# One reciprocal over all four groups in the cross-attention of a six-layer transformer stage, with the order of turns derived anew

## What is computed

```
def _L1_xcond_ref(x, noise_emb, context, src_mask, ctx_mask, ...):
    NL, D, H, DFF = (6, 128, 16, 512)
    ...
    def _attn(q, k, v, mask):
        scores = jnp.einsum('bqhd,bkhd->bhqk', q, k) / np.float32(np.sqrt(HD))
        scores = jnp.where(mask[:, None, None, :], jnp.float32(-jnp.inf), scores)
        w = jax.nn.softmax(scores, axis=-1)
        return jnp.einsum('bhqk,bkhd->bqhd', w, v)
    ...
    for i in range(NL):
        xn = _adaln(x, noise_emb, n1_w[i], n1_b[i])
        qkv = xn @ qkv_w[i].T
        ...
        a = _attn(q, k, v, src_mask).reshape(B, L, D) @ so_w[i].T
        x = x + a
        xn = _adaln(x, noise_emb, n2_w[i], n2_b[i])
        ...
        a = _attn(q, k, v, ctx_mask).reshape(B, L, D) @ co_w[i].T
        x = x + a
        xn = _adaln(x, noise_emb, n3_w[i], n3_b[i])
        h = jax.nn.gelu(xn @ f1_w[i].T + f1_b[i], approximate=False)
        x = x + (h @ f2_w[i].T + f2_b[i])
```

## Time and profile before

| | |
|---|---|
| time, median of three | 5061.23 us (5058.92 to 5063.93) |
| the profiled execution | 5061.74 us, span 5059.6 us |
| PE busy in the span | 4376.1 us (86%) |
| DVE busy | 3535.1 us (70%) |
| ACT busy | 2299.6 us (45%) |
| POOL busy | 376.5 us (7%) |
| the transformer stage | from 2121 to 3658 us, PE at a granted clock of 0.85 |

### The profile page before, as it was taken

One profiled execution on the slowest core, in us unless ns is written; L12 is line 12 of the kernel. 1 busy time (PEld: TensorE's weight loads), 2 busy tenths in 40 slices (PEclk: granted clock), 3 DMA queues, 4 the chain that ended last, 5 costly groups with the idle time before them and its releaser, 6 DMA issues. The chain is left out here.

```text
span 5059.6 us, 88974 instructions
## 1 busy us (share of the span) xinstructions
PE 4376.1 (86%) x25446; PEld 2749.6 (54%) x25446; DVE 3535.1 (70%) x17626; ACT 2299.6 (45%) x7385; POOL 376.5 (7%) x306
## 2 busy tenths in 40 slices
PE   8999999999999998488888888888623888997979
PEld 6888888888888886323333333333312553333456
DVE  7888888888888885476677777777445783443435
ACT  4555555555555553145555555555321112332313
POOL 0000000000000000201111111111001001221000
PEclk9999999999999998688888888888755897998679
DMA  0000000000000001222222222222000010000001
GB/s 28 2 2 2 2 2 2 2 2 2 2 2 2 2 2 30 56 53 45 49 45 49 45 49 45 49 45 47 15 8 0 29 34 14 9 7 13 17 1 38
DMA packets 82323, 106.79 MB, mean 21 GB/s; under 512 B 26095, under 2 KB 75434, under 8 KB 79915
## 3 DMA queue, kind: packets, MB, share of 16 engines
q1 hardware_dynamic: 81899, 101.85, 8.4%
HBM read 70.74 MB, written 30.26 MB: 20 GB/s over the span
## 5 line engine op out<-in xcount | busy, mean ns | idle before, releaser
L287 DVE CUSTOM_DVE_ANT_0 I-219junk<-I-215encw,I-218expo,I-227rec 128x77 f32<-128x77 f32 x3072 | 941.6, 357 | 6.2
L1315 DVE TENSOR_REDUCE I-41383nmax<-ps 128x1 f32<-128x512 f32 x768 | 501.4, 685 | 220.2 <-PE ps L984 213.6
L1203 ACT ACTIVATE I-41386prob<-ps 128x512 f32<-128x512 f32 x768 | 428.4, 596 | 229.8 <-PE ps L1021 227.1
L265 ACT ACTIVATE I-217tanh_s<-ps 128x77 f32<-128x77 f32 x1024 | 241.3, 236 | 595.5 <-PE ps L245 595.5
L245 PEld LDWEIGHTS ps<-I-212hist,I-49small 128*128 128x128 f32 x2048 | 305.0, 188 | 297.9 <-DVE I-212hist L323 297.8
L245 PE MATMUL ps<-I-212hist,I-49small 128*128 128x77 f32 x2048 | 456.6, 305 | 0.1
L251 PE MATMUL ps<-I-217tanh_s,I-49small 128*128 128x77 f32 x2048 | 454.5, 304 | 0.0
L984 PE MATMUL ps<-I-41377kS,I-41376qS 96*128 96x512 bf16 x768 | 332.1, 459 | 125.0 <-DVE I-41383nmax L1315 57.8
L247 PE MATMUL ps<-I-212hist,I-216uh_h 128*128 128x128 f32 x2048 | 439.9, 296 | 0.0
L252 PE MATMUL ps<-I-212hist,I-49small 128*128 128x128 f32 x2048 | 439.8, 296 | 0.0
L273 ACT ACTIVATE I-223hh<-I-229gate_t,I-228pre,I-222rh 128x1 f32<-128x1 f32 x1024 | 395.3, 386 | 84.5
(11 more groups left out here) (502 smaller groups left out, 7799.5 us busy)
## 6 DMA issues: line engine op xcount, KB each, us to landing
I-41376qS<-parts SPq DMA_DIRECT2D x24, 768.0 KB, 7.6
parts<-I-41395room SPq DMA_DIRECT2D x36, 384.0 KB, 2.5
parts<-I-41395room SPq DMA_DIRECT2D x36, 256.0 KB, 2.2
I-41377kS<-parts SPq DMA_DIRECT2D x12, 768.0 KB, 7.9
parts<-I-41395room SPq DMA_DIRECT2D x36, 128.0 KB, 1.8
I-49small<-in_layers SPq DMA_DIRECT2D x6, 768.0 KB, 9.0
I-41376qS<-I-41385mrow SPq DMA_DIRECT2D x192, 2.0 KB
I-41376qS<-I-41392crow SPq DMA_DIRECT2D x192, 2.0 KB
```

The lines of the kernel that those rows point to most:

```text
L287: return e.tensor_tensor_reduce(junk[:, 2 * g + b, :], encw[:, g, b, :], expo[:, b, :], inv[:, b:b + 1], rec[:, b, g:g + 1], ALU.mult, ALU ...
L1203: e.activation(prob[:, tau % 2, j, :], k.ps[:, b, :], ACT.Exp, scale=scale).then_inc(free[b], 1)
L1315: e.tensor_reduce(nmax[:, U % HG, i, j:j + 1], k.ps[:, use[0], :], AX.X, ALU.max, negate=True).then_inc(free[use[0]], 1)
```

## The change

It does three things. In the cross-attention all four groups are added on POOL (three additions), one reciprocal serves them, and the second reciprocal is gone. The multiplication of group 3 goes from DVE to POOL, after that of group 1. `cV` has the zero columns that this needs (six more MEMSETs, once, while the stage loads). And the five strings of `TURNS` are new (that of the self-attention's steps included, whose own arithmetic stays).

```
 e.wait_ge(s.zeroed, 2)
 for dst in (V, cV):
     for g in range(HG):
-        for n in range(HG - 1):
-            if n != g and g < HG - 1:
+        for n in range(HG):
+            if n != g and (dst is cV or n < HG - 1 and g < HG - 1):
                 e.memset(dst[:, :, 4 * g:4 * g + 4, 8 + n:9 + n], 0.0).then_inc(s.ones, 1)
...
     n = HG * (r - B) + g
     if g == 0:
-        e.wait_ge(s.csum, 2 * (r - B + 1))
+        e.wait_ge(s.csum, 3 * (r - B + 1))
         e.reciprocal(cinv[:], cinv[:]).then_inc(s.cinv, 1)
         yield
-    if g == HG - 1:
-        e.wait_ge(*done(R[r, ("a", g)]))
-        e.wait_ge(s.cwide, n)
-        e.reciprocal(cinv[:], co_in[:, g, :]).then_inc(s.cinv, 1)
-    e.wait_ge(s.cinv, 2 * (r - B) + 1 + g // (HG - 1))
+    e.wait_ge(s.cinv, r - B + 1)
     if n >= 2:
         e.wait_ge(s.cnormed, n - 1)
     e.stream_shuffle(cwide[:, g % 2, :], cinv[:], [8 + g] * 32).then_inc(s.cwide, 1)
-    if g != 1:
+    if g % 2 == 0:
...
-for g in range(1, HG - 1):
+for g in range(1, HG):
     e.wait_ge(*done(R[r, ("a", g)]))
     if g > 1:
-        e.wait_ge(s.csum, 2 * (r - B) + g - 1)
+        e.wait_ge(s.csum, 3 * (r - B) + g - 1)
         e.tensor_tensor(cinv[:], cinv[:], co_in[:, g, :], ALU.add).then_inc(s.csum, 1)
...
-e.wait_ge(s.cwide, N + 2)
-e.wait_ge(s.cnormed, N + 1)
-e.tensor_tensor(co_in[:, 1, :], co_in[:, 1, :], cwide[:, 1, :], ALU.mult).then_inc(s.cnormed, 1)
-yield
+for g in (1, 3):
+    e.wait_ge(s.cwide, N + g + 1)
+    e.wait_ge(s.cnormed, N + g)
+    e.tensor_tensor(co_in[:, g, :], co_in[:, g, :], cwide[:, g % 2, :], ALU.mult).then_inc(s.cnormed, 1)
+    yield
```

Of the strings, one line shows the kind of change (the middle part of DVE's; the rest has the same form):

```
-        "mmmrmmmmmrmmmmrraaaraaarrrmmmmrmrmrmmmmmmmmmmmmmmmmrrrrrrrrrmrrrrrmrrrrrmrmmmmmmmmmmmmrmrrmrmmrmmrmmrmmmmmmmm"
+        "mmrmmmmmmrrrraaaaaarmrrmmmmrmrmrmmmmmmmmmmmmmmmmmmmmrrrrrrrrrrrrrrrrrmrrrmmmmmmmmmmmmmmmmmmmrrrmrrmmmmrmrmmmmm"
```

79 lines of the change are left out of this document (39 added, 40 removed).

## The result

The changed kernel takes 5106.67 us (median of six runs, 5091.97 to 5124.38), the kernel before, run beside it, 5060.07 (six runs, 5036.54 to 5072.70). The ratio is 1.0097, with a 95% interval of 1.0069 to 1.0126: slower by one per cent. The forecast was 5091.6 in 5040 to 5118, slower with a chance of 0.58. The profiled execution took 5109.62 us with a span of 5107.9, 48.3 more than that of the kernel before.

The account below looks back on a forecast made before the run. No engine fills a piece; the ring of waits between streams bounds it. 2.7 - 1.6 - 1.3 - 0.7 + 4.0 = +3.1 us a piece, nine times, plus 1.9 at the last: 5061.7 + 30 = 5091.6, range 5040 to 5118.

Parts of the forecast that it names:

- E: Self-attention rounds 8 to 15: splits gathered before round 10's last exponential lengthen the stretch, +4.0 us a piece.
- rounds keep up: Rival at ACT, rounds 9 to 11: rounds keep up while splits run, -0.5 us or less there, total 5049; chance 0.25.
- A: Self-attention output product to first cross-attention maxima: four more units of m, bound by DVE's reduces, +2.7 us a piece.
- B: Cross-attention's maxima: three reduces of m moved ahead of it, -1.6 us a piece, bounds -2.05 and 0.
- D: Cross-attention's output product to round 8: two reduces of m where five stood, -0.7 us a piece.
- C: Cross-attention normalisation, fourth group's copy to output product's end: a chain of 13.0 us against 14.3, -1.3 a piece.
- POOL beside DVE: Normalisation, port shared with DVE: POOL's full-tile steps taken at 1.27 us, not stretched, by the earlier trace's row.
- What was taken as nothing: First pieces and a = 11, where only two streams run: 0, with 4 us either way in all.
- rival 3: Five last rounds of a piece: PE idles, granted clock falls to 0.50, +6 us a piece, total 5143; chance 0.08.
- DMA: Where pieces meet: q lands about 5 us before the norm, ending the 3.98 us PE gap; alone this saves nothing.

Follow-up runs that it names:

- e1: One reciprocal (new arithmetic) with the order of the kernel before, the reciprocal two units of m later at r = 12: 5115.81 us, ratio 1.0104.
- e2: The changed kernel's order with the old arithmetic of two reciprocals: 5158.51 us, ratio 1.0189.
- e9: e5 with the changed kernel's tail order (first norm to round 15, r = 3 to 11): 5103.53 us, ratio 1.0099.
- e10: e5 with four units of m put ahead of the first L1094 in seven pieces: 5080.48 us, ratio 1.0039.
- e12: e11 with two units of m behind the maxima, and in r = 2 a round before the first output product: 5053.14 us, ratio 0.9989.
- e11: e5 with r = 12 reordered on PE and the maxima's copy earlier on ACT in four r: 5056.82 us, ratio 1.0000.
- e5: One reciprocal in the old order, changed only from the last product with the values to the output product's end: 5063.46 us, ratio 1.0013.

## Why the prediction was right, and where it was not

- **The time and its sign** were right: 5106.67 in 5040 to 5118, slower as forecast. Of +46.6 us the sum had 30, and the miss was within the range by width, not by reasoning: nine pieces took 1.2 us each more than forecast, the start and the end of the stage 15 more, and the unchanged part behind it happened to be 7 shorter. The reason given was half of the matter: the expected gain of the arithmetic and the expected price of the order were taken as two things that stand side by side. e1 and e2 show that they are one.
- **E** (+4.0 forecast, +4.1 measured) had the place and the size right, and e9 shows the tail's order by itself (+4.1 between rounds 8 and 15, +4.6 a piece). The sum has some luck in it. Rounds 8 to 10 were forecast at 14.4 us and took 11.3 and 14.3 by turns, 12.8 in the mean; rounds 10 to 15 were forecast at 14.6 and took 16.4 and 15.7. And the splits are only a part: ACT also waits 2.27 us for the maxima's transposes, where it did not wait before. That the rival "rounds keep up" was wrong, the 6.9 us between rounds 8 and 9 show, against 3.7 before.
- **A** (+2.7, measured +2.0) was right in mechanism: e10 gives 0.65 a unit, and from the norm's transposes to first L1094 it is 3.0 us more (23.45 against 20.45). It was too large because it held that the norm could not come before its 4.8 us. It could: with q landed it comes at 4.08, 1.0 earlier in the mean. Below 19 units the DMA is the floor (e12).
- **B** (-1.6, measured -0.9): the size was taken near its bound of three reduces. Where the rest went was not followed in the traces, and the same holds for **D** (-0.7, measured -1.1).
- **C** was the step that failed (-1.3, measured 0.0). It added up the chain and took the engines on it to be free. The bound named one of the two losses ("late by one (0.7)") and left it out of the sum; the other, PE at a weighting when POOL is done (0.75), it did not have. The chain itself was sized about right: in e11, where little stands in its way, C is 13.4 to 13.6 in most pieces, against 13.0. Larger than its miss in the sum: that the new chain, without any change of order, would cost 5.8 was not seen.
- **POOL beside DVE.** The sum went by the row that POOL's 1.27 us are not stretched, and the changed kernel bears that out (min/median/max of the additions and of the multiplications). The last section shows where they do hold each other up.

```profile
L1535 POOL TENSOR_TENSOR I-41394cinv<-I-41394cinv,I-41395room x24: 1261/1270/1282, 2292.5 to 3679.7; 128x512 f32<-128x512 f32 x24
```

```profile
L1545 POOL TENSOR_TENSOR I-41395room<-I-41395room,I-41393cwide x24: 1267/1273/1282, 2304.0 to 3689.4; 128x512 f32<-128x512 f32 x24
```

- **What was taken as nothing**: the start of the stage (+5.2) and the pieces at its end (+9.4 beside the +2.2 of the last normalisation, forecast 1.9) were put at 0 with 4 us either way; together they are 14.6, outside that. Their order was changed too and was not costed. And from round 15 to the end of the output product it is 0.5 more, above all in every other piece, where the product's end runs at the clock's lower level.
- **The clock** (rival 3) fell in a place where it had been at 1.00, but only for 3.4 us in every other piece and not in the five last rounds. Nor did the missing gap at the meeting of pieces give any back: the stretches at 0.50 there are 10.2 and 23.9 us long, as in most pieces before, and a piece has 35.0 us at the lower level against 33.4.
- **DMA**: q's landing was read right from the earlier trace rows. That its going would bring nothing beyond filled gaps was wrong by the 1.0 us in A.

## What to carry to other kernels

When an edit lengthens one link of a chain in lists that issue in order, cost the work that stands behind that link on each engine, not the link: here a reciprocal that starts 3.7 us later (2.0 behind the fourth copy in e1, 1.7 ahead of it before) became 5.8 us in C, with two rounds on PE between the late products. Mend the order at that place first, in the one stage that changed (e5), before anything else is moved; a whole order made anew bought the same stage at 4.6 us elsewhere. And test arithmetic and order apart in both directions: here neither alone was cheaper than both together, and one reading, that the one loses and the other gains, fell at once.
